# State-space rounds in a new order on all four engines, with the softplus head on ScalarE and the shift by columns

## The chip, the cores and the metric

The kernel runs on one core of a Trainium2 chip. The metric is device time in microseconds. A core has five engines that run side by side, each in the order of its own instruction list: TensorE (PE; PEld is its weight load), VectorE (DVE), ScalarE (ACT), GpSimd (POOL) and SyncE (SP, which issues the DMAs). They meet only at semaphores.

## The reference

Four stages follow each other, each with a layernorm in front and a residual behind: an attention-like recurrence over 32 sequences of 256 tokens and 128 features, a feed-forward net, a state-space block, and the feed-forward net again. The change concerns the state-space block, and the helper that ends a layernorm's statistics.

```python
zxbcdt = hidden_states @ W_in
z = zxbcdt[..., :D_INNER]
xBC = jax.nn.silu(_causal_dwconv(xBC, conv_w, conv_b))
...
dt = jax.nn.softplus(dt + dt_bias)
A = -jnp.exp(A_log)
y = _ssd(x, dt, A, Bm, Cm) + x * D[None, None, :, None]
y = y * jax.nn.silu(z)
y = y * jax.lax.rsqrt(jnp.mean(y * y, axis=-1, keepdims=True) + EPS) * norm_w
return y @ W_out
```

`_ssd` multiplies scores (products of the B and C features, times the exponential of a difference of running sums of dt*A) with x*dt, head by head. The depthwise convolution has 4 taps.

## The kernel before

The tokens stand in SBUF as 16 groups of 512 (4 tiles of 128). Every engine's program is written out by hand: stage by stage a function `space_half` (and `attention_half`, `ffn_half`) per engine lists what the engine does in one round. The order on an engine is the order of the code, and nothing reorders it.

**The state-space stage** has 16 rounds, h = 1 to 16. Round h works on three groups at once: b = h (projection and convolution), e = h - 1 (decays, scores, x*dt) and f = h - 2 (output, residual). Up to round 8 to 11 it also does the layernorm of a group x seven rounds ahead, turns it feature-major (`turn`), and projects dt for a group d = h + 6. The lines (of before) that matter:

- PE: `gate` L1974 (z), `conv` L1970, `log_decay` L1988 and L1990 (two fp16 matmuls: exponent of the decay, called ld below with head and batch), `head_outputs` L2001 (16 matmuls, called hy 0 and hy 1 for the two halves of the heads), `token_major` L2009, `transposes_of` L1645, `of_token` L1872 (dt), `steps_to_rows` L1962, `products` L2015, `mean_squares` L2023, `out_of` L2030.
- DVE: `stats_at` L1088 to L1093, `shift_at` L1100, `with_bias` L1401 (sets `z_done`), `taps` L1503 (three adds onto what ACT began), `times_dt` L1520, `skip` L1510, `mean_square` L1529, `add_residual` L1392 (the residual: 4 instructions), and the softplus chain of 64 columns for four groups at once (a quad), L1417 to L1452.
- ACT: `first_tap` L973 (begins a convolution block), `silu_x` L979, `silu_z` L984, `square_y` L989, `decay_of` L994, `products_out` L1000, `normalise_of` L823, `feature_major_of` L815, `exp_of_quad` L967. Two table loads a round, ahead of L994 and of L984.
- POOL: `score_of` L721 (4 a round), `gated_y` L727 (2), the sum of squares L768, `ln_rstd_of` L609 and L612, the rms root L777, and for a quad `diffs` (L739 to L745) and `split_sums` (L756 to L761).

The residual needs `out_of` (PE) and the root (POOL). The next round's hy 0 needs the residual, since both use the PSUM bank `y_bank[0]`. `skip(e, r)` needs hy r; `gated_y` needs `skip`; `square_y` needs `gated_y`.

**A quad's chain** runs over four rounds. In rounds 1, 5 and 9 `softplus_begin` makes -|z| and max(z, 0) on DVE, ACT takes the exponential, and `softplus_middle`, `_series` and `_end` follow on DVE. In rounds 2, 6 and 10 PE turns the steps (`steps_to_rows`, which waits for the end of the softplus chain and for this round's `with_bias`), DVE takes chunk sums (L1464; `products` waits for them, as they share `mid_bank[1]`), and POOL takes six steps of `diffs`. In rounds 3, 7 and 11 DVE runs two scans (`running_sums`, L1475 and L1476), and POOL six steps of `split_sums`.

`shift_at` is called in the attention stage as well, once for each of its groups:

```python
nc.vector.scalar_tensor_tensor(shift[u][:, :], mv[u][:, :, 0], -1.0, rstd[u][:, :],
                               ALU.mult, ALU.mult).then_inc(shift_done, 1)
```

## Time and profile before

| what | value |
|---|---|
| median of 3 runs | 834.76 us (832.9 to 836.47) |
| the profiled execution | 835.77 us, its span 833.7 us, mean granted clock 0.953 |
| busy: PE, DVE, ACT, POOL | 746.8, 619.6, 531.0, 556.2 us |
| attention, then feed-forward | until some 300 us, then until some 430 us |
| state-space rounds | some 430 to 735 us |
| second feed-forward | to the end |

The span runs from the first to the last instruction; the time has 2.07 us more around it. Busy time is what the profile draws; PE's is drawn too long, since the modelled end of a matmul lies behind the start of the next. A row of the timeline reads: start, length, engine, line, operation, names, shape, count, and in brackets how long the engine was idle before it and who ended that.

### The profile page before, as it was taken

The page shows a single profiled execution, that of the slowest core. Times are in us where ns is not written, and L with a number is a line of the kernel's source. Part 1 is how long each engine was busy: PE and PEld are TensorE (multiplying, and loading weights), DVE is VectorE, ACT ScalarE, POOL GpSimd, SP SyncE. Part 2 cuts the span into 40 slices and gives each one's busy share as a digit, 9 for nine tenths or more (in the row PEclk, how much of TensorE's full clock was granted, in tenths as well). Part 3 has the DMA queues.
Part 4 walks back from the last instruction along what each step waited for, and adds up shares of the span by engine and source line. Part 5 has one row for each costly group of instructions (what it writes and reads, how often), then busy time and mean ns, then how long its engine had stood idle before and what let it go on. Part 6 is the DMA issues. An engine that isn't in the chain of part 4 may idle for free. (4 is left out here: it accounts for less than half of the span.)

```text
span 833.7 us, 15931 instructions
## 1 busy us (share of the span) xinstructions
PE 746.8 (90%) x5114; PEld 547.7 (66%) x5114; DVE 619.6 (74%) x1728; ACT 531.0 (64%) x1023; POOL 556.2 (67%) x920
## 2 busy tenths in 40 slices
PE   3589999999999897999779799899979999979997
PEld 2578888888888775666644566566645565546665
DVE  3568877787788548888568787887888777668885
ACT  3244344434543236988548788788978688848886
POOL 1567666776677504777724697588758876777775
PEclk9689999999999899999759899999999999999999
DMA  4341131112111102000200000000000000000112
GB/s 126 82 134 46 50 77 34 30 30 48 39 30 30 29 15 102 0 1 0 78 3 7 1 1 9 1 1 5 7 1 1 9 1 1 1 1 27 51 51 77
DMA packets 59996, 25.83 MB, mean 31 GB/s; under 512 B 22288, under 2 KB 59152, under 8 KB 59664
## 3 DMA queue, kind: packets, MB, share of 16 engines
q1 hardware_dynamic: 59920, 24.90, 11.2%
q8 instruction: 37, 0.61, 0.3%
q14 instruction: 39, 0.32, 0.1%
HBM read 15.26 MB, written 9.63 MB: 30 GB/s over the span
## 5 line engine op out<-in xcount | busy, mean ns | idle before, releaser
L1503 DVE SCALAR_TENSOR_TENSOR arena<-bank,convw_sb,arena 128x510 f32<-128x510 f32 (+2 forms) x192 | 142.5, 745 | 31.9 <-ACT arena L973 27.2
L721 POOL TENSOR_TENSOR arena<-arena 128x768 f32<-128x768 f32 x64 | 114.8, 1814 | 12.8 <-ACT arena L1000 12.6
L701 POOL TENSOR_TENSOR arena<-ff,arena 128x512 f16<-128x512 f32 x64 | 73.6, 1159 | 28.7 <-ACT arena L938 26.6
L1970 PE MATMUL bank<-xnT,win_sb 128*128 128x512 f32 x128 | 73.9, 661 | 2.7 <-DVE arena L1503 2.7
L632 POOL TENSOR_TENSOR leafV<-leafV,leaf_tmp 32x14 f32<-32x14 f32 (+6 forms) x224 | 62.4, 278 | 17.6
L830 ACT ACTIVATE ff<-bank 128x256 f32<-128x256 f32 (+2 forms) x80 | 34.0, 424 | 57.6 <-PE bank L1658 35.3
L1324 DVE SCALAR_TENSOR_TENSOR ff<-bank,ff 128x512 f32<-128x512 f32 x96 | 64.5, 684 | 7.3 <-ACT ff L933 6.3
L933 ACT ACTIVATE ff<-bank 128x512 f32<-128x512 f32 x96 | 56.2, 587 | 18.4 <-PE bank L1886 18.0
L815 ACT ACTIVATE xnT<-bank 128x512 f32<-128x512 f32 x34 | 20.3, 597 | 73.3 <-PE bank L1645 73.3
L628 POOL TENSOR_TENSOR leaf_tmp<-leafV 32x14 f32<-32x14 f32 (+6 forms) x224 | 55.8, 249 | 16.4
L994 ACT ACTIVATE arena<-bank 128x384 f32<-128x384 f32 x128 | 59.8, 492 | 9.3 <-PE bank L1990 8.5
L2001 PE MATMUL bank<-arena 128*64 128x256 f32 (+1 forms) x512 | 49.7, 338 | 17.8 <-DVE x_all L1392 17.8
L727 POOL TENSOR_TENSOR arena<-arena 128x512 f32<-128x512 f32 x30 | 37.7, 1268 | 39.6 <-DVE arena L1510 39.4
L1128 DVE SCALAR_TENSOR_TENSOR arena<-bank,arena 128x256 f32<-128x256 f32 (+1 forms) x128 | 44.6, 411 | 25.8 <-PE bank L1732 15.7
L2001 PEld LDWEIGHTS bank<-arena 128*64 128x64 f32 x512 | 32.4, 139 | 45.3 <-DVE x_all L1392 22.9
L973 ACT ACTIVATE arena<-bank,convb_sb,convw_sb 128x512 f32<-128x512 f32 x64 | 49.9, 781 | 18.9 <-PE bank L1970 18.9
L823 ACT ACTIVATE xn<-x_all,shift,rstd 128x128 f32<-128x128 f32 x112 | 45.9, 481 | 11.4 <-DVE shift L1100 11.4
L692 POOL TENSOR_SCALAR xn<-x_all,pair_rstd,pair_shift 128x128 f32<-128x128 f32 x76 | 34.7, 467 | 23.2 <-DVE pair_shift L1299 20.4
L979 ACT ACTIVATE arena<-arena 128x512 f32<-128x512 f32 x64 | 38.6, 632 | 17.9 <-DVE arena L1503 17.9
L1988 PE MATMUL bank<-ff,slabs 128*128 128x384 f16 x128 | 41.0, 331 | 3.8 <-ACT arena L994 3.7
L938 ACT ACTIVATE arena<-ff 128x512 f16<-128x512 f32 x64 | 39.9, 623 | 6.1 <-DVE ff L1324 6.1
L1885 PE MATMUL bank<-xh,gate 128*128 128x512 f16 x96 | 36.8, 384 | 4.8 <-DVE x_all L1392 3.0
(216 smaller groups left out, 2162.5 us busy)
## 6 DMA issues: line engine op xcount, KB each, us to landing
LT_dram<-arena SPq DMA_DIRECT2D x16, 256.0 KB, 2.3
ff<-R_dram SPq DMA_DIRECT2D x16, 256.0 KB, 2.8
out<-x_all SPq DMA_DIRECT2D x8, 512.0 KB, 3.2
x_all<-in_L_attn_a_x SPq DMA_DIRECT2D x7, 512.0 KB, 5.6
slabs<-in_tables SPq DMA_DIRECT2D x2, 1024.0 KB, 6.0
ff<-in_tables SPq DMA_DIRECT2D x2, 768.0 KB, 4.3
x_all<-in_L_attn_a_x SPq DMA_DIRECT2D x2, 256.0 KB, 3.7
R_dram<-tab SPq DMA_DIRECT2D x2, 256.0 KB, 6.7
```

The lines of the kernel that those rows point to most:

```text
L628: nc.gpsimd.tensor_tensor(prod, V[:, s:s + 1, s + 1:LEAF].broadcast_to([leaf_rows, s, below]), V[:, 0:s, s:s + 1].broadcast_to([leaf_rows, ...
L632: nc.gpsimd.tensor_tensor(V[:, 0:s, s + 1:LEAF], V[:, 0:s, s + 1:LEAF], prod, ALU.subtract).then_inc(leaf_step, 1)
L701: nc.gpsimd.tensor_tensor(of_block(hl[u], j), hidT[u][:, j, :], of_block(hh[u], j), ALU.subtract).then_inc(hl_done[u], 1)
L721: nc.gpsimd.tensor_tensor(score[h], cb[g % 2], hgam[h], ALU.mult).then_inc(score_done, 1)
L823: last = nc.scalar.activation(xn[u][:, cols(t)], x_all[:, n % GROUPS * GROUP + t * P:n % GROUPS * GROUP + (t + 1) * P], ACT.Identity, scal ...
L933: nc.scalar.activation(silu_g[u][:, j, :], bank[u][(1, 3, 1)[j]][:, :], ACT.Silu, scale=DEQUANT).then_inc(silu_done[u], 1)
L973: nc.scalar.activation(xbc[r][b % 2], conv_bank[r % 2][:, :], ACT.Identity, scale=convw_sb[:, r, TAPS - 1:TAPS], bias=convb_sb[:, r:r + 1] ...
L994: nc.scalar.activation(hgam[h][:, batch * TRI:(batch + 1) * TRI], step_bank[batch][:, 0:TRI], ACT.Exp).then_inc(hgam_done, 1)
L1324: nc.vector.scalar_tensor_tensor(hidT[u][:, j, :], bank[u][(2, 0, 2)[j]][:, :], DEQUANT, silu_g[u][:, j, :], ALU.mult, ALU.mult).then_inc( ...
L1503: nc.vector.scalar_tensor_tensor(acc_of[:, :, s:SEQ], src_of[:, :, 0:SEQ - s], convw_sb[:, r, TAPS - 1 - s:TAPS - s], acc_of[:, :, s:SEQ], ...
L1970: mm(conv_bank[r % 2][:, :], win_sb[:, INNER + r * P:INNER + (r + 1) * P], xnT[b % XNT_SETS][:, :], start=True, stop=True).then_inc(conv_m ...
L2001: last = mm(y_bank[r][k * HEAD_DIM:(k + 1) * HEAD_DIM, batch * SEQ + c * P:(batch + 1) * SEQ], x_of[:, 2 * batch + c, h * HEAD_DIM:(h + 1) ...
```

## The change

In the state-space rounds, each engine's list is put in another order. Three instructions change their kind: -|z| and max(z, 0) of a quad become |z| (with the sign in the exponential's scale) and a Relu on ACT; `softplus_begin` leaves DVE's round. `shift_at` becomes four one-column instructions, everywhere it is called. The prologue keeps the old way for quad 0, and everything outside `space_half` and `shift_at` stays, but for the order of three SiLU operations ahead of the rounds.

```diff
 # POOL, space_half
                 if f is not None:
                     gated_y(f, 1)
+                if x is not None:
+                    ln_rstd_of(*x)
...
                 if e is not None:
                     score_of(e, 0)
-                    score_of(e, 1)
                 if f is not None:
                     pool.wait_ge(ms_done, done(f))
...
                 if e is not None:
+                    score_of(e, 1)
                     score_of(e, 2)
 # ACT
+            def softplus_begin(q):
+
+                act.wait_ge(z_done, done(QUAD * (q + 1) - 1))
+                act.wait_ge(chain_step, CHAIN * q)
+                nc.scalar.activation(nabs_dt[:, :], z_dt[q % 2][:, :], ACT.Abs).then_inc(chain_step, 1)
+                nc.scalar.activation(relu_dt[:, :], z_dt[q % 2][:, :], ACT.Relu).then_inc(chain_step, 1)
+                act.wait_ge(chain_step, CHAIN * q + 1)
+                nc.scalar.activation(e_dt[:, :], nabs_dt[:, :], ACT.Exp, scale=-1.0).then_inc(e_done, 1)
 # ACT, space_half: its whole order now
                     silu_x(e, 0)
                     silu_x(e, 2)
                     silu_x(e, 3)
+                if b is not None:
+                    first_tap(b, 0)
                 if turn is not None:
                     feature_major_of(*turn, mid_bank[0])
...
                     decay_of(e, 0, 1)
+                    decay_of(e, 0, 0)
                 if f is not None:
                     square_y(f, 0)
+                if e is not None:
+                    decay_of(e, 1, 1)
+                if exp_q is not None:
+                    softplus_begin(exp_q)
+                if e is not None:
+                    products_out(e, 1)
+                if f is not None:
                     square_y(f, 1)
...
                     silu_z(b, 1)
-                    first_tap(b, 3)
+                    silu_z(b, 0)
                     silu_x(b, 1)
-                    silu_z(b, 0)
 # DVE, shift_at
-                nc.vector.scalar_tensor_tensor(shift[u][:, :], mv[u][:, :, 0], -1.0, rstd[u][:, :],
-                                               ALU.mult, ALU.mult).then_inc(shift_done, 1)
+                for t in range(GROUP_TILES):
+                    last = nc.vector.tensor_scalar(shift[u][:, t:t + 1], rstd[u][:, t:t + 1], mv[u][:, t, 0:1], -1.0,
+                                                   ALU.mult, ALU.mult)
+                last.then_inc(shift_done, 1)
 # DVE, space_half
-                if begin_q is not None:
-                    softplus_begin(begin_q)
                 if chunk_q is not None:
                     chunk_sums(chunk_q)
-                if sums_q is not None:
-                    running_sums(sums_q)
...
+                if e is not None:
+                    times_dt(e, 0)
                 if f is not None:
                     mean_square(f)
-                if e is not None:
-                    times_dt(e, 0)
+                if sums_q is not None:
+                    running_sums(sums_q)
                 if b is not None:
                     taps(b, 2)
```

On PE a round now reads: gate 0, conv 0, hy 0, token-major 1, turn, ld(0,1), hy 1, ld(0,0), `of_token`, `steps_to_rows`, conv 1, ld(1,1), products 1, ld(1,0), products 0, ld(2,1), gate 1, conv 2, ld(2,0), token-major 0, ld(3,1), mean squares, ld(3,0), conv 3, `out_of`. Before, it read: gate 0, ld(0,1), hy 0, conv 0, hy 1, token-major 1, turn, ld(0,0), conv 1, `of_token`, `steps_to_rows`, ld(1,1), products 1 and 0, ld(1,0), ld(2,1), mean squares, gate 1, ld(2,0), token-major 0, conv 2, ld(3,1), ld(3,0), `out_of`, conv 3.

**DVE in round 5**, from the last group of taps ahead of the residual. Names are those of the program (`arena` holds the stage's tiles, `x_all` the tokens). Before:

```order
L1432 TENSOR_SCALAR dt_acc<-dt_w 128x64
L1439 SCALAR_TENSOR_TENSOR dt_acc<-dt_acc,dt_w 128x64 x3
L1392 SCALAR_TENSOR_TENSOR x_all<-bank_2,arena,x_all 128x128 x4
L1503 SCALAR_TENSOR_TENSOR arena<-bank_1,convw_sb,arena 128x2x255
L1503 SCALAR_TENSOR_TENSOR arena<-bank_1,convw_sb,arena 128x2x254
L1503 SCALAR_TENSOR_TENSOR arena<-bank_1,convw_sb,arena 128x2x253
L1439 SCALAR_TENSOR_TENSOR dt_acc<-dt_acc,dt_w 128x64 x3
L1446 SCALAR_TENSOR_TENSOR dt_acc<-dt_acc,dt_w 128x64
L1448 SCALAR_TENSOR_TENSOR dt_dt<-dt_acc,dt_relu 128x64
L1452 TENSOR_TENSOR dt_dA<-dt_dt,aneg_row 128x8x2x4
L1510 SCALAR_TENSOR_TENSOR arena<-arena,skip_col,bank_2 128x512
L1510 SCALAR_TENSOR_TENSOR arena<-arena,skip_col,bank_3 128x512
```

The same place with the change (residual L1403, taps L1514, `skip` L1521, `times_dt` L1531, series L1450):

```order
L1443 TENSOR_SCALAR dt_acc<-dt_w 128x64
L1521 SCALAR_TENSOR_TENSOR arena<-arena,skip_col,bank_2 128x512
L1531 TENSOR_TENSOR arena<-bank_3,dt_dt 128x4x128
L1450 SCALAR_TENSOR_TENSOR dt_acc<-dt_acc,dt_w 128x64 x6
L1457 SCALAR_TENSOR_TENSOR dt_acc<-dt_acc,dt_w 128x64
L1459 SCALAR_TENSOR_TENSOR dt_dt<-dt_acc,dt_relu 128x64
L1463 TENSOR_TENSOR dt_dA<-dt_dt,aneg_row 128x8x2x4
L1521 SCALAR_TENSOR_TENSOR arena<-arena,skip_col,bank_3 128x512
```

The whole chain now stands behind the residual and the last taps; its second part stands between `skip(e, 0)` and `skip(e, 1)`.

**ACT at the start of a plain round.** `bank_0` and `bank_1` are PSUM banks. Before, `first_tap(b, 0)` (L973) stands behind the squares and three decays:

```order
L994 ACT_TABLE_LOAD
L994 ACTIVATE arena<-bank_1 128x384
L815 ACTIVATE xnT<-bank_2 128x512
L989 ACTIVATE arena<-arena 128x512 x2
L994 ACTIVATE arena<-bank_0 128x384
L994 ACTIVATE arena<-bank_1 128x384
L973 ACTIVATE arena<-bank_0,convb_sb,convw_sb 128x512
L1000 ACTIVATE arena<-bank_3 128x384
```

With the change (`silu_x` L989, `first_tap` L983, `feature_major_of` L816, `decay_of` L1004):

```order
L994 ACTIVATE arena<-bank_3 128x512
L994 ACTIVATE arena<-bank_2 128x512
L989 ACTIVATE arena<-arena 128x512 x4
L983 ACTIVATE arena<-bank_0,convb_sb,convw_sb 128x512
L816 ACTIVATE xnT<-bank_2 128x512
L1004 ACT_TABLE_LOAD
```

`first_tap(b, 0)` now stands ahead of the table load, the decays and the squares.

**PE in round 6**, around `steps_to_rows` (L1962 before, L1971 with the change). Before:

```order
L1970 MATMUL bank_1<-xnT,win_sb 128x512
L1872 MATMUL bank_3<-win_sb,xnT 128x4 x4
L1962 MATMUL bank_3<-tab,dt_dA 32x128 x2
L1988 MATMUL bank_1<-ff,slabs 128x384
L1990 MATMUL bank_1<-never,ident 128x2x128
L2015 MATMUL bank_3<-arena 128x256
```

With the change:

```order
L1881 MATMUL bank_3<-win_sb,xnT 128x4 x4
L1971 MATMUL bank_3<-tab,dt_dA 32x128 x2
L1979 MATMUL bank_1<-xnT,win_sb 128x512
L1997 MATMUL bank_1<-ff,slabs 128x384
L1999 MATMUL bank_1<-never,ident 128x2x128
L2024 MATMUL bank_3<-arena 128x256
```

The convolution block 1 moved from ahead of `of_token` to behind `steps_to_rows`, that is behind its wait and ahead of the products.

## Rows read from the trace of the kernel before

**Rows 1.** Residuals of rounds 2, 5, 6, 7, 8 and 15: timeline of DVE

```profile
476.75 1.12 DVE L1392 SCALAR_TENSOR_TENSOR x_all<-bank,arena,x_all 128x128 f32<-128x128 f32 x4
...
534.75 1.12 DVE L1392 SCALAR_TENSOR_TENSOR x_all<-bank,arena,x_all 128x128 f32<-128x128 f32 x4
...
555.14 1.12 DVE L1392 SCALAR_TENSOR_TENSOR x_all<-bank,arena,x_all 128x128 f32<-128x128 f32 x4
...
574.39 1.12 DVE L1392 SCALAR_TENSOR_TENSOR x_all<-bank,arena,x_all 128x128 f32<-128x128 f32 x4
...
593.01 1.12 DVE L1392 SCALAR_TENSOR_TENSOR x_all<-bank,arena,x_all 128x128 f32<-128x128 f32 x4
...
720.64 0.60 DVE L1392 SCALAR_TENSOR_TENSOR x_all<-bank,arena,x_all 128x128 f32<-128x128 f32 x2
```

**Rows 2.** Stretch, length, busy (count) of PE PEld DVE ACT POOL, clock, DMA

```profile
687.04:703.84 16.80, 16.00 (x101) 10.05 (x100) 12.39 (x22) 13.80 (x25) 11.99 (x9) 1.00 0.01 1
...
574.39:593.01 18.62, 17.26 (x112) 11.46 (x112) 14.37 (x33) 16.03 (x30) 16.71 (x17) 1.00 0.04 11
514.02:534.75 20.73, 17.00 (x112) 11.47 (x112) 18.38 (x43) 18.79 (x36) 15.10 (x12) 1.00 0.01 2
...
651.30:670.24 18.94, 17.20 (x100) 10.59 (x99) 12.47 (x22) 13.37 (x24) 16.53 (x16) 0.91 0.04 10
```

**Rows 3.** Timeline of round 8, from the residual before it on

```profile
576.26 0.39 POOL L756 CAST pieces<-ff 32x256 f16<-32x256 f32 x1
...
578.07 1.52 PE L2001 MATMUL bank<-arena 128*64 128x256 f32 x16
579.64 0.75 DVE L1510 SCALAR_TENSOR_TENSOR arena<-arena,skip_col,bank 128x512 f32<-128x512 f32 x1 [1.26 <-PE bank L2001]
580.41 2.49 POOL L727 TENSOR_TENSOR arena<-arena 128x512 f32<-128x512 f32 x2
...
580.90 0.87 DVE L1088 BATCH_NORM_STATS2 stats<-x_all 128x6 f32<-128x128 f32 x4
...
582.93 0.63 ACT L989 ACTIVATE arena<-arena 128x512 f32<-128x512 f32 x1 [0.59 <-POOL arena L727]
...
584.21 0.78 ACT L973 ACTIVATE arena<-bank,convb_sb,convw_sb 128x512 f32<-128x512 f32 x1
...
585.02 2.31 DVE L1503 SCALAR_TENSOR_TENSOR arena<-bank,convw_sb,arena 128x510 f32<-128x510 f32 x3 [2.28 <-ACT arena L973]
```

**Rows 4.** Timeline of DVE and PE in rounds 5 and 6

```profile
532.42 1.15 DVE L1428 TENSOR_TENSOR dt_w<-dt_e,dt_rec 128x64 f32<-128x64 f32 x1
...
534.09 0.74 DVE L1439 SCALAR_TENSOR_TENSOR dt_acc<-dt_acc,dt_w 128x64 f32<-128x64 f32 x3
...
535.92 1.64 PE L2001 MATMUL bank<-arena 128*64 128x256 f32 x16 [3.68 <-DVE x_all L1392]
...
537.49 2.08 PE L1970 MATMUL bank<-xnT,win_sb 128*128 128x512 f32 x2
```

**Rows 5.** Timeline of POOL and DVE at the start of round 11

```profile
634.74 0.59 POOL L739 TENSOR_TENSOR ff<-ff 32x248 f32<-32x248 f32 x1
...
639.36 2.48 POOL L727 TENSOR_TENSOR arena<-arena 128x512 f32<-128x512 f32 x2
639.42 2.96 DVE L1475 TENSOR_TENSOR_SCAN ff<-ones_col,ff 32x256 f32<-32x256 f32 x1
```

**Rows 6.** The shift's line: durations ns min/median/max, first and last start

```profile
L1100 DVE SCALAR_TENSOR_TENSOR shift<-mv,rstd x28: 152/154/1165, 6.4 to 627.0; 128x4 f32<-128x4 f32 x28
```

**Rows 7.** Timeline of an attention round

```profile
209.04 0.28 DVE L1093 BATCH_NORM_AGGREGATE mv<-stats 128x2 f32<-128x6 f32 x3
...
210.80 0.15 DVE L1100 SCALAR_TENSOR_TENSOR shift<-mv,rstd 128x4 f32<-128x4 f32 x1
...
213.45 0.71 PE L1714 MATMUL bank<-ff,arena 128*128 128x128 f32 x4 [0.21 <-DVE arena L1170]
```

**Rows 8.** Who waited for DVE's L1170: us, times

```profile
  PE bank L1714: 2.9, 13
```

More of the change, by code:

```diff
@@ L2052, in space_half @@
                     gate(e, 0)
-                    if e > 0:
-                        quad_landed(e)
-                        log_decay(e, 0, 1)
+                if b is not None:
+                    pe.wait_ge(xnT_done, done(2 * GROUPS + b))
+                    conv(b, 0)
                 if f is not None:
@@ L2072, in space_half @@
                     if e > 0:
-                        log_decay(e, 0, 0)
-                if b is not None:
-                    conv(b, 1)
+                        quad_landed(e)
+                        log_decay(e, 0, 1)
+                if f is not None:
+                    pe.wait_ge(ms_done, past(f - 1))
+                    head_outputs(f, 1)
+                if e is not None and e > 0:
+                    log_decay(e, 0, 0)
                 if d is not None:
@@ L2084, in space_half @@
                     steps_to_rows(rows_q)
+                if b is not None:
+                    conv(b, 1)
                 if e is not None:
```

74 lines of the change are left out of this document (35 added, 39 removed).

## The prediction

> **What bounds the kernel now.** I read the page first: PE is busy 746.8 of 833.7 us (the table above). That is an average over stages with different limits, so I went on by stage, first to the stretches between residuals, then to the timeline of one round. The state-space rounds are measured from residual to residual: 476.75 to 720.64 us for the thirteen rounds 3 to 15, that is 243.9 us [rows 1]. Several kinds are seen there. A light round (13 to 15: no layernorm, no turn, no dt) takes 16.80 us with all engines partly idle: PE busy 16.00, ACT 13.80, DVE 12.39, POOL 11.99 [rows 2]. A full round takes 18.62 us (round 8), rounds 5 and 6, which carry the softplus chain, take 20.7 and 20.4, and round 7 takes 19.25 [rows 1, 2].
>
> The timeline of round 8 shows what sets the period [rows 3]. DVE waits twice: 1.26 us for the second head outputs before `skip(e,1)`, and 2.28 us for ACT's first tap before its own taps. The chain between the two is hy 1 (1.52), `skip` (0.75), two gated products on POOL (2.49), the square, two decays and the first tap on ACT (from 582.93 to 584.99), and from there DVE works without a gap to the residual (585.02 to 593.01 + 1.12), whose end releases hy 0. So the loop is residual, hy 0, conv, hy 1, skip, POOL, square, decays, first tap, taps, residual. No engine is full; a loop through all four is the bound. In round 8 POOL came late: it was at its six split steps from 576.26 and began the products only at 580.41, both at once, after `skip(e,1)`. Had the first been done by then, as in a round without split steps, the loop would be one product (1.25) shorter, some 17.4.
>
> The attention stage is another matter. In 13 rounds PE waits for DVE's L1170, 2.9 us in all and 0.21 in the round shown, and otherwise runs without a gap [rows 7, 8]. DVE works without a gap from the bias adds through the shift to L1170. So there every nanosecond added at the shift is added to the round.
>
> **The change part by part.**
>
> *First tap early (ACT), conv 0 ahead of hy 0 (PE).* The first tap no longer hangs on the square. It follows `silu_x(e,3)`, which needs the last taps (2.3 us behind the residual): ready at 2.25 + 0.63 + 0.78 = 3.7 us behind the residual's end, where DVE reaches its taps only after `skip(e,1)`, at 4.2 + 0.75 + 1.4 (statistics, 0.87 and the aggregates, and bias) = 6.35. The wait of 2.28 us is gone. Laid out from the residual's end with the durations above, DVE then needs 15.0 us for a full round. What is late next is PE: its list of a light round holds 16.00 us of drawn busy time [rows 2], of which tails of 0.07 to 0.16 at its five or six gaps are drawn too long; counted start to start I get 15.6, and 16.9 for a full round (17.26 drawn). The bounds are 15.2 and 16.0. I take 15.6 and 16.9. ACT (13.80 and 16.03 drawn) fits under both.
>
> So the thirteen rounds are laid out again, one by one, to be set against their 243.9.
>
> *Light rounds 13 to 15:* 15.6 each instead of 16.8, 46.8 in all. *Round 12* was 18.94, with the clock at 0.91 and POOL late by the split [rows 2]; with PE dense it goes to 15.7.
>
> *Rounds 4 and 8 (split steps on POOL):* these take 4.1 us (from 576.26 to the products at 580.41 [rows 3]) behind the last scores, and push the gated products, which are no longer in front of the taps. Behind a round as late as 3 and 7 below, PE starts at once: 16.7 and 16.6 (round 8 was 18.62).
>
> *Rounds 5 and 9:* 20.73 now [rows 2] in round 5, where -|z| and the chain's first half stand ahead of the residual. All of it leaves this round. ACT gets |z| and Relu, two of 64 columns, for which I take 0.25 each (a DVE instruction of that size takes that [rows 4]); products and gate 1 come 0.5 later, which PE's list hides; without that cover it would be 0.5 a round. 16.9 each.
>
> *Rounds 6 and 10:* the chain has only moved. The middle (five instructions, 1.55 us), six series steps and three of the end (nine at 0.25, 2.3 us; three take 0.74 [rows 4]), and one hold of 0.75 by POOL's gated product now lie in front of `skip(e,1)`: it starts at 8.1 instead of 4.2. Then statistics, bias at 10.2, and only then `steps_to_rows`, with conv 1 now between it and the products. PE is idle from 6.2 to 10.3. At the start of round 6 PE was idle 3.68 us, and the convolution behind the head outputs took 2.08 us, twice its usual time, at the lower of the two clock levels, 1.2 instead of 2.4 GHz [rows 4]. I expect the same fall here: conv 1 until 12.5, decay and products 14.4 instead of 7.1. From there the round is as usual, 9.2 to the residual: 23.6, where round 6 took 20.4. Without the fall of the clock it is 21.7.
>
> *Rounds 3, 7 and 11:* the scores end later on POOL (one more stands behind the root), so the six steps of `diffs` (4.6 us, 634.74 to 639.36 [rows 5]) end at 7.4, the gated products at 10.0, and now the first square stands ahead of a decay that gate 1 hangs on: everything comes 2.8 later. The running sums have moved from a place where DVE waited to one just ahead of the taps before the residual: 1.3 us, and up to 2.3 more if POOL holds them, as in round 11, where a scan of 0.65 took 2.96 behind two POOL instructions [rows 5]. I take 1.0 of hold (the root's length). 20.3 (round 3: 20.2, round 11, which has no dt and no statistics: 19.9), where round 7 took 19.25.
>
> *Sum over the rounds:* 20.2 + 16.7 + 16.9 + 23.6 + 20.3 + 16.6 + 16.9 + 23.6 + 19.9 + 15.7 + 46.8 = 237.2, against 243.9: 6.7 less. Rounds 1, 2 and 16 have a hold less on DVE and the same loops over a shorter way; I take 1.3 for them, an estimate. For waits that such a layout doesn't see I take off 0.6: **7.4 gained.** The bounds are 0 (another loop takes the place) and 16 (no fall of the clock, no hold).
>
> *The shift by columns.* In the state-space rounds, where a score runs on POOL, the shift takes up to 1.17 us instead of 0.15 [rows 6]. Four columns with one tensor input each may escape the hold. DVE no longer bounds these rounds, so this is hidden by PE's list; without that cover it would be up to 1.0 a round. In the attention rounds there is no hold and no cover. No row shows a one-column instruction with a per-partition operand. The nearest are the three small aggregates that take 0.28 us together where one takes 0.15 [rows 7]: each further one costs 0.065. Four columns then cost 0.2 more than one instruction, 13 times: **2.6 us lost.** From below nothing, if they cost no more than the one; from above 4 x 0.154 - 0.154 = 0.46, 13 times, 6.0.
>
> The Trainium skill (VectorE: DVE Perf Modes, "The DRAIN you can't avoid") says that the next Vector instruction does not start until the pipe of the last is empty. By it four columns cost four whole instructions, the 6.0 of the upper bound, and the whole sum would be a gain of 1.4. The rows at 0.065 apart speak against it.
>
> **Sum:** 7.4 - 2.6 = 4.8 us. The profiled execution goes from 835.77 to 831.0 (833.7 to 828.9 in its span); it is 1.0 above the median of 834.76, so the median goes to 830.0.
>
> **Rivals.**
> 1. *The clock does not fall and the scans are not held* (rounds 2, 6 and 10; 3, 7 and 11). For it: a round is full of matmuls on both sides of the idle time. Against it: that time is 4.1, longer than the 3.68 that it fell after. It gives 1.9 x 3 + 1.0 x 3 = 8.7 more: 821.
> 2. *The columns run one after another:* 6.0 in place of 2.6: 833.4. Against it the rows above, for it that page.
> 3. *POOL's loop takes the place of the one removed.* One score more stands behind the root, and the fourth score is needed by hy 1 of the next round; I find it done 0.4 us before that. If POOL's waits for the mean square are longer, the rounds stay as they are, and the columns cost 2.6: 837.4.
> 4. *Slower.* In rounds 2, 6 and 10 the chain in front of `skip(e,1)` meets holds at each of its three starts (a product of 64 columns took 1.15 instead of 0.25 [rows 4]), 2.0 more, and the idle PE falls to the low level for the products, gate and decays behind them too, 2.2 more: 4.2 x 3 = 12.6, 842.6. It decides from 3.0 us a round on; POOL, which is idle until `skip(e,0)`, speaks against the holds.
>
> **How the numbers follow.** A run of three resolves about 0.5% of this kernel, 4.2 us: faster is below 830.6, slower above 838.9. The forecast has 0.45 (its own range 826 to 834, half of it on each side of 830.6, a little more on the fast side), rival 1 0.20, rival 2 0.08, rival 3 0.10, rival 4 0.17. Faster: 0.26 + 0.20 = 0.46. Slower: 0.17. Same: 0.37. The range of 821 to 840 leaves out half of rival 1 and most of rival 4.
>
> **What would show it.** In the profile after: no wait for L983 (first tap) ahead of the first taps; light rounds of 15.6 with PE's idle time near nothing; rounds 5 and 9 near 17; round 6 and 10 near 23.6 with a lower clock, PE idle before `steps_to_rows`; round 7 at 20 with a first scan over 0.65; PE's wait for L1170's successor in attention at 0.41. The prediction is wrong if the light rounds stay at 16.8, if attention loses more than 4 us or nothing, or if round 6 is near 20.

## The result and the profile after

The changed kernel takes 831.86 us (median of 18 runs), the kernel before 836.62 beside it: a ratio of 0.9923, 95% interval 0.9905 to 0.9941. The ratio leaves out two of the 18 that ran in a slower state. The change makes the kernel faster by 0.6 to 0.95%. The forecast was 830.0, from 834.76: a gain of 4.8, and 4.8 is what the two medians give.

From the page of the changed kernel: its engines, and the group of the taps (columns: busy us, mean ns | idle time before it, and what ended most of that):

```profile
span 825.8 us, 16018 instructions
PE 738.0 (89%) x5114; PEld 545.4 (66%) x5114; DVE 618.8 (75%) x1806; ACT 529.0 (64%) x1029; POOL 557.7 (68%) x920
L1514 DVE SCALAR_TENSOR_TENSOR arena<-bank,convw_sb,arena 128x510 f32<-128x510 f32 (+2 forms) x192 | 142.5, 743 | 21.0 <-ACT arena L983 16.4
```

The span is 7.9 us shorter, and the page doesn't say where. (The profiled execution, 827.91 us, lies 4.0 below the median of its kernel and the one before 0.9 below its own, so 3.1 of the 7.9 belong to this pair of executions.) The residuals do, here those of rounds 2 and 15 in the timeline of DVE (before: [rows 1]):

```profile
482.53 1.12 DVE L1403 SCALAR_TENSOR_TENSOR x_all<-bank,arena,x_all 128x128 f32<-128x128 f32 x4 [0.56 <-PE bank L2142]
...
712.54 1.13 DVE L1403 SCALAR_TENSOR_TENSOR x_all<-bank,arena,x_all 128x128 f32<-128x128 f32 x4 [0.56 <-PE bank L2142]
```

The thirteen rounds take 230.0 us instead of 243.9, so 13.9 less; round 2's residual comes 5.8 later than before; the last two stretches of the stage together are 0.3 longer (26.75 instead of 26.46). 13.9 - 5.8 - 0.3 = 7.8, all but 0.1 of the 7.9. The 5.8 are lost before the state-space rounds begin. Rounds 4, 5, 6, 7, 8, 10 and 15 by window (columns as in [rows 2]):

```profile
501.31:518.47 17.16, 16.51 (x111) 11.38 (x112) 14.17 (x37) 14.87 (x29) 16.05 (x16) 1.00 0.05 11
518.47:535.07 16.60, 16.60 (x113) 11.48 (x112) 14.17 (x36) 16.01 (x33) 13.57 (x11) 1.00 0.01 1
535.07:557.71 22.64, 18.68 (x115) 12.39 (x114) 19.09 (x52) 15.80 (x30) 13.15 (x11) 0.92 0.00 1
557.71:576.51 18.80, 17.91 (x114) 11.46 (x112) 15.25 (x38) 16.70 (x31) 17.77 (x18) 1.00 0.00 1
576.51:593.68 17.17, 16.52 (x111) 11.39 (x112) 14.16 (x36) 14.87 (x29) 16.06 (x16) 1.00 0.05 11
...
610.28:630.61 20.33, 16.32 (x107) 10.71 (x106) 18.92 (x51) 15.81 (x30) 13.17 (x11) 1.00 0.00 1
...
697.05:712.54 15.49, 15.44 (x101) 10.06 (x100) 12.57 (x22) 13.82 (x25) 12.01 (x9) 1.00 0.00 1
```

In rounds 5 and 15 PE is busy for the whole window: it is the bound there. In round 6 it is not, and its clock is down (0.92). Round by round, in us from residual to residual, for all kernels of this study (each from one profiled execution; unchanged rounds repeat to 0.05 us between executions, but those in which the clock falls differ by up to 1.3):

| kernel | 3 | 4 | 5 | 6 | 7 | 8 | 9 | 10 | 11 | 12 | 13-15, mean | sum |
|---|---|---|---|---|---|---|---|---|---|---|---|---|
| before | 18.7 | 18.6 | 20.7 | 20.4 | 19.3 | 18.6 | 20.7 | 19.2 | 18.4 | 18.9 | 16.80 | 243.9 |
| predicted | 20.2 | 16.7 | 16.9 | 23.6 | 20.3 | 16.6 | 16.9 | 23.6 | 19.9 | 15.7 | 15.6 | 237.2 |
| changed | 18.8 | 17.2 | 16.6 | 22.6 | 18.8 | 17.2 | 16.6 | 20.3 | 18.4 | 17.0 | 15.49 | 230.0 |
| cols_alone | 18.3 | 18.5 | 20.7 | 21.3 | 18.3 | 18.5 | 20.7 | 18.0 | 19.6 | 16.9 | 16.80 | 241.0 |
| tap_early | 18.7 | 18.6 | 20.8 | 21.3 | 18.9 | 18.6 | 20.8 | 19.2 | 17.2 | 16.9 | 16.08 | 239.2 |
| tap_rstd | 18.1 | 18.0 | 20.9 | 20.4 | 18.6 | 17.8 | 20.9 | 19.4 | 17.1 | 16.9 | 16.09 | 236.2 |
| tap_rstd_cols | 18.1 | 17.8 | 21.1 | 20.4 | 18.6 | 17.8 | 21.1 | 19.4 | 17.1 | 16.9 | 16.09 | 236.4 |
| whole_shift | 19.5 | 17.8 | 16.6 | 24.0 | 19.5 | 17.8 | 16.6 | 20.3 | 18.4 | 17.1 | 15.49 | 234.0 |
| cols_space | 18.8 | 17.2 | 16.6 | 22.8 | 18.8 | 17.2 | 16.6 | 20.3 | 18.5 | 17.1 | 15.49 | 230.2 |
| conv0_late | 18.8 | 17.2 | 17.1 | 24.0 | 18.8 | 17.2 | 17.1 | 20.3 | 18.4 | 17.1 | 15.74 | 233.1 |
| conv1_first | 18.8 | 17.2 | 16.8 | 23.0 | 18.8 | 17.2 | 16.8 | 22.0 | 18.4 | 17.0 | 15.49 | 232.4 |
| chain_split | 18.8 | 17.2 | 21.3 | 19.9 | 18.8 | 17.2 | 21.3 | 18.1 | 18.4 | 17.0 | 15.49 | 234.4 |
| sums_first | 23.3 | 16.6 | 16.6 | 23.9 | 21.4 | 17.4 | 16.6 | 20.9 | 24.2 | 15.7 | 15.49 | 243.0 |
| tap_late | 25.0 | 18.9 | 22.4 | 25.1 | 22.6 | 19.7 | 19.1 | 26.2 | 19.4 | 24.3 | 19.25 | 280.5 |
| bias_early | 18.8 | 17.2 | 16.6 | 20.5 | 18.8 | 17.2 | 16.6 | 21.1 | 18.4 | 17.1 | 15.49 | 228.7 |

How large that is, round 6 shows. sums_first changes nothing in it, and in whole_shift the shift isn't held there (0.15 us at 544.70) and is followed by a wait of 2.24 for ACT. Yet both take 1.3 more than the changed kernel, at a lower mean clock, 0.86 for 0.92. Round 6 of whole_shift, then of sums_first:

```profile
529.99:553.95 23.96, 20.00 (x115) 13.26 (x114) 18.78 (x48) 15.81 (x30) 13.17 (x11) 0.86 0.00 1
539.19:563.11 23.92, 19.96 (x115) 13.20 (x114) 19.18 (x51) 15.79 (x30) 13.17 (x11) 0.86 0.00 1
```

conv0_late has 23.98 at 0.86 too, cols_space 22.77 at 0.93. So a difference of 1.3 in round 6 is no sign of what an edit does.

The attention stage went the other way. The shift's line, durations as in [rows 6], and an attention round in the timelines of DVE and PE:

```profile
L1110 DVE TENSOR_SCALAR shift<-rstd,mv x112: 201/203/215, 6.4 to 624.4; 128x1 f32<-128x1 f32 x112
```

```profile
113.06 0.57 DVE L1110 TENSOR_SCALAR shift<-rstd,mv 128x1 f32<-128x1 f32 x4
113.54 0.70 DVE L1164 STREAM_TRANSPOSE ff<-ff 128x512 f32<-128x512 f32 x1
...
115.53 0.41 DVE L1181 TENSOR_TENSOR arena<-arena,bank 128x256 f32<-128x256 f32 x1
...
116.00 0.71 PE L1723 MATMUL bank<-ff,arena 128*128 128x128 f32 x4 [0.37 <-DVE arena L1181]
...
133.04 0.71 PE L1723 MATMUL bank<-ff,arena 128*128 128x128 f32 x4 [0.37 <-DVE arena L1181]
```

and in the kernel before, at the same place of its round [rows 7]:

```profile
212.99 0.41 DVE L1170 TENSOR_TENSOR arena<-arena,bank 128x256 f32<-128x256 f32 x1
```

A column takes 0.203 us, the next begins 0.12 behind it, four take 0.57 where one instruction took 0.15. From the shift's start to that of the instruction PE waits for it is 2.47 us (113.06 to 115.53) instead of 2.19 (210.80 to 212.99): of the 0.42 that the columns add, 0.28 arrive, since the transpose and the reduction behind them take 0.13 less; why they do stays open. PE's wait is 0.37 instead of 0.21 [rows 7], and a round takes 17.04 us (116.00 to 133.04) instead of 16.76. From the first to the last of the thirteen waits, twelve rounds, it is 204.9 us, where the kernel before took 201.1: 3.8 lost, 0.65 in the first round and 0.28 to 0.29 in each other.

### The profile page after: what moved, and what is told of

Same layout as the page of the kernel before. It is cut to its first block and busy times, and to the rows that moved or that the text cites. A ratio compares the mean times of both kernels' runs of the same rounds, so it can differ in the third digit from the quotient of the medians.

```text
span 825.8 us, 16018 instructions
## 1 busy us (share of the span) xinstructions
PE 738.0 (89%) x5114; PEld 545.4 (66%) x5114; DVE 618.8 (75%) x1806; ACT 529.0 (64%) x1029; POOL 557.7 (68%) x920
## 5 line engine op out<-in xcount | busy, mean ns | idle before, releaser
L1514 DVE SCALAR_TENSOR_TENSOR arena<-bank,convw_sb,arena 128x510 f32<-128x510 f32 (+2 forms) x192 | 142.5, 743 | 21.0 <-ACT arena L983 16.4
L1979 PE MATMUL bank<-xnT,win_sb 128*128 128x512 f32 x128 | 71.8, 644 | 3.4 <-DVE arena L1514 3.3
L1004 ACT ACTIVATE arena<-bank 128x384 f32<-128x384 f32 x128 | 61.2, 492 | 17.5 <-PE bank L1999 17.2
L934 ACT ACTIVATE ff<-bank 128x512 f32<-128x512 f32 x96 | 56.2, 587 | 18.2 <-PE bank L1895 17.8
L983 ACT ACTIVATE arena<-bank,convb_sb,convw_sb 128x512 f32<-128x512 f32 x64 | 49.6, 774 | 25.5 <-PE bank L1979 21.3
L1139 DVE SCALAR_TENSOR_TENSOR arena<-bank,arena 128x256 f32<-128x256 f32 (+1 forms) x128 | 44.6, 411 | 25.8 <-PE bank L1741 15.6
L816 ACT ACTIVATE xnT<-bank 128x512 f32<-128x512 f32 x34 | 20.1, 594 | 64.9 <-PE bank L1654 64.9
L727 POOL TENSOR_TENSOR arena<-arena 128x512 f32<-128x512 f32 x30 | 37.8, 1269 | 23.3 <-DVE arena L1521 23.1
L1660 PE MATMUL bank<-ff,arena 128*128 128x64 f32 x256 | 36.2, 288 | 6.5 <-DVE ff L1164 6.5
```

The lines of the kernel that those rows point to most:

```text
L934: nc.scalar.activation(silu_g[u][:, j, :], bank[u][(1, 3, 1)[j]][:, :], ACT.Silu, scale=DEQUANT).then_inc(silu_done[u], 1)
L983: nc.scalar.activation(xbc[r][b % 2], conv_bank[r % 2][:, :], ACT.Identity, scale=convw_sb[:, r, TAPS - 1:TAPS], bias=convb_sb[:, r:r + 1] ...
L1004: nc.scalar.activation(hgam[h][:, batch * TRI:(batch + 1) * TRI], step_bank[batch][:, 0:TRI], ACT.Exp).then_inc(hgam_done, 1)
L1514: nc.vector.scalar_tensor_tensor(acc_of[:, :, s:SEQ], src_of[:, :, 0:SEQ - s], convw_sb[:, r, TAPS - 1 - s:TAPS - s], acc_of[:, :, s:SEQ], ...
L1979: mm(conv_bank[r % 2][:, :], win_sb[:, INNER + r * P:INNER + (r + 1) * P], xnT[b % XNT_SETS][:, :], start=True, stop=True).then_inc(conv_m ...
```

## The experiments

All of them compute the whole reference.

**cols_alone** and **whole_shift**: the columns alone, and everything but the columns. **cols_space**: the changed kernel with columns in the state-space stage only.

```diff
 # cols_space, shift_at of the changed kernel
+                if n < 2 * GROUPS:
+                    nc.vector.scalar_tensor_tensor(shift[u][:, :], mv[u][:, :, 0], -1.0, rstd[u][:, :],
+                                                   ALU.mult, ALU.mult).then_inc(shift_done, 1)
+                    return
                 for t in range(GROUP_TILES):
```

> The kernel before, with the shift by columns and nothing else of the change. Theory (the new order gives the gain, the columns cost): the period of the attention rounds goes from 16.76 to 17.05 us, as in the changed kernel (+3.7 over 13 rounds); in the state-space rounds the column form isn't held by GpSimd, so that rounds 3 to 10, where the shift lies on the loop, get 0 to 0.6 shorter each (2 in all): the span 1 to 3 us longer than before. Rival (the gain comes from the holds that the columns avoid): the state-space rounds get over 5 us shorter in all and the span shorter than before.

> The changed kernel with the shift as one instruction everywhere, as before the change. Theory: attention rounds back at 16.76 us, 3.7 to 4 us less; in the state-space rounds the shift is held by GpSimd again, up to 1 us a round, which TensorE's list hides for the most part: 0 to 2 us more. The span 2 to 4 us shorter than that of the changed kernel. Rival (the holds matter): state-space rounds 0.5 us longer each, no gain.

> The changed kernel with the columns in the state-space rounds alone, one instruction in the attention stage. Theory: attention rounds at 16.76 us, state-space rounds as in the changed kernel (light 15.5, full 16.6), so the span is 3.7 to 4 us shorter than that of the changed kernel, and the time 0.987 to 0.989 of before. Rival (the 0.285 us a round in attention come from something else in the change, the time of the statistics or a DMA): attention stays at 17.05.

cols_alone: 841.33 us, ratio 1.0049 (1.0017 to 1.0082). whole_shift: 827.72, ratio 0.989 (0.9848 to 0.9932). cols_space: 826.52, ratio 0.9877 (0.9844 to 0.991). From the first to the last of the thirteen waits in attention it is 204.91 in the first and 201.10 in the other two: the columns cost 3.8 there in whatever order. In the state-space rounds cols_alone is 2.9 shorter than the kernel before, but 2.1 of that lie in round 12, where the clock stays at 1.00 instead of 0.91. The rival, that the avoided holds are the gain, fell. In the new order one whole instruction instead of four columns costs 0.65 to 0.67 in each of rounds 3, 4, 7 and 8, 2.65 in all; the 1.3 in round 6 are the clock's (above). With the 3.8 of attention that would make whole_shift 1.2 shorter than the changed kernel; the interval of its four runs holds 0.9923 and doesn't decide it. In round 8 of whole_shift, first DVE, then POOL:

```profile
584.78 1.23 DVE L1109 SCALAR_TENSOR_TENSOR shift<-mv,rstd 128x4 f32<-128x4 f32 x1 [1.58 <-POOL rstd L612]
```

```profile
583.72 1.03 POOL L612 TENSOR_TENSOR rstd<-var_eps,half_neg 128x4 f32<-128x4 f32 x1
584.73 1.26 POOL L771 TENSOR_TENSOR arena<-arena 128x512 f32<-128x512 f32 x1
```

The shift waits for POOL's reciprocal deviation (`rstd`) and is let go as POOL starts on its next instruction, the sum of squares (L771). The two end together (586.01 and 585.99): the shift is held for all of that, 1.23 instead of 0.15. The columns take 0.58 at the same place (587.88 in the changed kernel, behind the same wait of 1.58).

**tap_early, tap_rstd, tap_rstd_cols**: the kernel before, with the first tap moved; then the reciprocal deviation ahead of the sum of squares as well; then the columns in the state-space stage too.

```diff
 # ACT (tap_early and on)
                     silu_x(e, 3)
+                    if b is not None and e > 0:
+                        first_tap(b, 0)
...
-                if b is not None and e != 0:
-                    first_tap(b, 0)
 # POOL (tap_rstd and on)
                     gated_y(f, 1)
+                if x is not None:
+                    ln_rstd_of(*x)
+                if f is not None:
                     pool.wait_ge(ysq_done, done(INNER_BLOCKS * f + 1))
                     nc.gpsimd.tensor_tensor(ysq[0][f % 2], ysq[0][f % 2], ysq[1][f % 2], ALU.add).then_inc(ysum_done, 1)
-                if x is not None:
-                    ln_rstd_of(*x)
```

> The kernel before, with first_tap(b, 0) moved on ScalarE to right behind the three SiLU, and nothing else of the change. Theory (the loop through the gated products, the square and this tap sets the period): light rounds go from 16.80 to 16.0 to 16.2 us (not 15.5, since conv 0 still stands behind the first head outputs), round 8 from 18.62 to 17.5, and the span gets 7 to 10 us shorter, as much as by the whole change or more, since neither the columns' cost nor the longer softplus round come with it. Rival (TensorE's new order is needed as well): light rounds stay over 16.5 and the span within 3 us of before.

> The kernel before with two moves: the first tap of block 0 right behind the SiLUs of x on ScalarE, and the layernorm's reciprocal deviation ahead of the sum of squares on GpSimd. The tap alone gave light rounds of 16.08 but left full rounds at 18.60, where the shift waited 1.10 us for that reciprocal and was then held 1.77 us by a score. Theory (two things stood behind the tap's wait, the place of the reciprocal and GpSimd's hold): the wait of 1.10 is gone, the shift of one instruction is still held; rounds 4 and 8 go from 18.6 to 17.5 to 18.2, light rounds stay at 16.08, sum of rounds 3 to 15 some 234 to 237. Rival (the loop through GpSimd and the square bounds the full rounds): they stay at 18.6.

> tap_rstd with the shift by columns in the state-space rounds alone. Theory: the hold is gone as well, full rounds 4 and 8 reach the 17.2 of the changed kernel, rounds 5 and 9 stay longer than its 16.6 since the softplus chain is still split, sum some 232 to 235; nearly the whole gain of the change is then in three of its moves. Rival (the rest of the new order carries the full rounds): 18 or more.

tap_early: 836.21 us, ratio 0.9992 (0.9967 to 1.0017). tap_rstd: 831.03, ratio 0.9935 (0.9904 to 0.9965). tap_rstd_cols: 833.91, ratio 0.9953 (0.992 to 0.9987), not to be told from tap_rstd. tap_early missed its forecast of 7 to 10 us: its thirteen rounds gain 4.7, and its runs show 2.8 at most. Some of the 4.7 is lost just ahead of them: from the statistics in round 1 to round 2's residual (440.11 to 478.01) it is 37.9 us at a mean clock of 0.86, where the kernel before took 35.4 at 0.90. With the tap alone the light rounds fall to 16.08, but round 8 stays at 18.6. In its timeline of DVE the wait of 2.28 for the tap [rows 3] is gone, and another has come:

```profile
584.68 2.30 DVE L1503 SCALAR_TENSOR_TENSOR arena<-bank,convw_sb,arena 128x510 f32<-128x510 f32 x3
588.09 1.77 DVE L1100 SCALAR_TENSOR_TENSOR shift<-mv,rstd 128x4 f32<-128x4 f32 x1 [1.10 <-POOL rstd L612]
```

The taps start 8.4 us into the round instead of 10.6. But they end at 586.98, and then come 1.10 of waiting and a shift of 1.77. In the kernel before it had no wait there and took 0.74 (587.25), so 2.1 of the 2.2 that were won are used up. The same place with tap_rstd:

```profile
582.55 2.30 DVE L1504 SCALAR_TENSOR_TENSOR arena<-bank,convw_sb,arena 128x510 f32<-128x510 f32 x3
584.77 0.15 DVE L1101 SCALAR_TENSOR_TENSOR shift<-mv,rstd 128x4 f32<-128x4 f32 x1
585.89 2.31 DVE L1504 SCALAR_TENSOR_TENSOR arena<-bank,convw_sb,arena 128x510 f32<-128x510 f32 x3 [0.97 <-ACT arena L974]
```

The shift has neither wait nor hold, though it is still one instruction, and so the columns have nothing left to give. That part of the theory, a hold that only the columns lift, fell. What the changed kernel has beyond that, 0.6 in light rounds, 0.7 in round 8 and 4.3 in rounds 5 and 9, belongs to the rest of the new order; the same rest costs 0.6 in round 3, 2.3 in round 6, 1.0 in round 10 and 1.3 in round 11.

**conv0_late** and **conv1_first**: on PE, conv 0 behind hy 0 again; conv 1 ahead of `of_token` and `steps_to_rows` again.

```diff
 # conv1_first, PE
+                if b is not None:
+                    conv(b, 1)
                 if d is not None:
...
                     steps_to_rows(rows_q)
-                if b is not None:
-                    conv(b, 1)
```

> The changed kernel with the first convolution of a round behind the first head outputs again, as before. Theory (light rounds of 15.49 have PE full because the convolution fills the time in which PE would wait for the residual): light rounds go to some 16.1, what tap_early alone reached, and PE's idle time before the first head outputs is 0.6 a round; full rounds, which wait on DVE, change by less than 0.3. Rival (the early tap alone fills PE, the place of the convolution is worth nothing): 15.5.

> The changed kernel with the second convolution ahead of the dt product and the turned steps, where PE waits idle in rounds 2, 6 and 10. Theory: in round 6 PE's wait of 3.04 us before the steps is shortened by the convolution's 0.96 at full clock or 1.9 at the lower clock level, round 6 goes from 22.64 to 20.7 to 21.7 and round 2 alike; the others stay within 0.2; median 1 to 3 us below the changed kernel's 831.9. Rival (that round is bound by DVE's list behind the chain, not by PE's work behind the steps): 22.6 as before.

conv0_late: 830.61 us in a single run, too little to set beside the changed kernel's median. PE waits 0.36 for the residual ahead of hy 0 in light rounds (669.10), and these take 15.74, between theory and rival: the place of conv 0 is worth 0.25 of the 0.6, and 0.35 come from the rest of the new order, which I didn't take apart. Rounds 5 and 9 take 0.5 more, so the place matters there too; the 1.3 more in round 6 are no sign of it (above). conv1_first: 831.86 us, ratio 0.9939 (0.9906 to 0.9971), the same as the changed kernel and against the theory: round 6 takes 22.97 instead of 22.64, and round 10 22.03 instead of 20.33. Round 10 in its timeline of PE, its start being 612.00:

```profile
621.39 0.38 PE L1971 MATMUL bank<-tab,dt_dA 128*32 128x128 f32 x2 [2.27 <-DVE dt_dA L1463]
...
623.80 1.28 PE L2024 MATMUL bank<-arena 128*128 128x256 f32 x4 [1.77 <-issue]
```

and in the changed kernel, from 610.28 on:

```profile
619.64 0.38 PE L1971 MATMUL bank<-tab,dt_dA 128*32 128x128 f32 x2 [3.11 <-DVE dt_dA L1463]
619.86 1.02 PE L1979 MATMUL bank<-xnT,win_sb 128*128 128x512 f32 x2
...
622.05 0.89 PE L2024 MATMUL bank<-arena 128*128 128x256 f32 x4 [0.90 <-issue]
```

```profile
621.27 0.69 DVE L1475 TENSOR_TENSOR_SCAN ff<-tab,bank 32x128 f32<-32x128 f32 x2
```

The products start 11.8 us into the round in both. In the code they wait for DVE's chunk sums (L1475), and in both they start 0.09 behind the end of these (621.96 here, 623.71 in conv1_first), though the profile names no releaser. So conv 1 costs nothing where it was put. Moved out, it leaves PE idle for another 0.9 ahead of the products, and the granted clock is 0.54 from 624 to 626 and 0.61 from 626 to 628, where it stays at 1.00 in the changed kernel: the products take 1.28 instead of 0.89. The loss in round 10 is that of the clock. That the place of conv 1 decides it isn't shown: tap_late aside, six kernels have conv 1 and the chain in this round where the changed kernel has them, and in four of them the clock stayed at 1.00 (20.33 or 20.34), in two it fell (sums_first 20.88 and bias_early 21.11, both at 0.92).

**chain_split**: the chain's middle and three of its steps on DVE ahead of the residual again.

```diff
+                if begin_q is not None:
+                    softplus_middle(begin_q)
+                    softplus_series(begin_q, 0, 3)
                 if f is not None and b is not None:
                     add_residual(f)
...
                 if begin_q is not None:
-                    softplus_middle(begin_q)
+                    softplus_series(begin_q, 3, 6)
+                    softplus_end(begin_q)
...
-                if begin_q is not None:
-                    softplus_series(begin_q, 0, 6)
-                    softplus_end(begin_q)
```

> The changed kernel with the middle and three steps of the softplus chain ahead of the residual again, the other three steps and the end behind it, as before; |z| and Relu stay on ScalarE. Theory (the chain only moved, but behind the residual it lies in front of the turned steps, where it makes PE idle long enough for the clock to fall): rounds 5 and 9 get some 2.3 longer (16.6 to 18.9), round 6 gets 2.3 shorter and another 1.0 to 1.5 since the clock stays (22.64 to some 19), round 10 gets 2.3 shorter (20.33 to 18); sum of rounds 3 to 15 within 2 us of 230.0, on the short side. Rival (the chain ahead of the residual costs more there than behind, since PE, ScalarE and GpSimd all wait for the residual): rounds 5 and 9 near 20.7 as before, the sum 3 or more longer.

838.49 us, ratio 1.0024 (0.9999 to 1.005). Rounds 5 and 9 take 4.7 more, 6 and 10 only 2.8 and 2.2 less. DVE at the end of round 5, and PE right behind it:

```profile
537.56 1.17 DVE L1439 TENSOR_TENSOR dt_w<-dt_e,dt_rec 128x64 f32<-128x64 f32 x1
538.77 1.73 DVE L1441 TENSOR_TENSOR dt_w<-dt_w 128x64 f32<-128x64 f32 x1
```

```profile
542.60 2.83 PE L2011 MATMUL bank<-arena 128*64 128x256 f32 x16 [4.15 <-DVE x_all L1403]
```

Ahead of the residual two small products are held for 2.4 us behind POOL's scores (535.06 to 540.41). In the changed kernel, behind the residual, they took 0.22 and 0.23 (539.42 and 539.68). And PE waits 4.15 for the late residual and runs the head outputs at the low clock, 2.83 where they take 1.52. The rival stands: the chain's place is worth 4.4 us in the thirteen rounds. By the runs (1.0024 beside 0.9923) the whole is more, some 8 us; rounds 1 and 2, which carry a quad's chain too, took 2.4 more in this execution, which is no more than executions differ by there, and the rest isn't placed.

**sums_first** and **tap_late**: the running sums ahead of the first taps again; the first tap behind the second square again, everything else as changed.

```diff
 # sums_first, DVE
+                if sums_q is not None:
+                    running_sums(sums_q)
                 if b is not None:
                     taps(b, 0)
...
-                if sums_q is not None:
-                    running_sums(sums_q)
```

> The changed kernel with the two scans of the running sums ahead of the first taps again, as before, instead of behind the mean square. Theory (in the new order DVE has no idle time in these rounds ahead of its taps, so the 1.34 us of scans cost their length at either place): rounds 3, 7 and 11 within 0.3 of 18.79, 18.80 and 18.41. Rival (the scans' old place is a place where DVE waits, their new one is on the path to the residual): 0.5 to 1.3 shorter.

> The changed kernel with the first tap of block 0 on ScalarE behind the second square again, all else as changed. Theory (the early tap is the move that the others need, since without it the loop through hy 1, the products on GpSimd, the square and the tap sets every round): light rounds 16.8 or longer, since one more decay, the softplus head and a products' copy now stand ahead of the square, full rounds 18.6 or longer, sum 243 or more. Rival (the other moves carry a part of the gain alone): light rounds 16.1 to 16.5, sum 235 to 240.

sums_first: 841.26 us in a single run, and both theories were wrong: rounds 3, 7 and 11 take 4.5, 2.6 and 5.7 more. DVE and POOL in its round 7:

```profile
571.44 2.96 DVE L1486 TENSOR_TENSOR_SCAN ff<-ones_col,ff 32x256 f32<-32x256 f32 x1 [0.39 <-POOL ff L745]
```

```profile
570.69 0.72 POOL L745 TENSOR_TENSOR ff<-ff 32x256 f32<-32x256 f32 x1
571.37 2.48 POOL L727 TENSOR_TENSOR arena<-arena 128x512 f32<-128x512 f32 x2
```

A scan that waits for POOL's last step is let go just as POOL begins its two gated products, and is held through both. The whole round is 2.6 longer. In the new place, behind the mean square, all four scans of this line take 0.669 us (573.14 in round 7). POOL's root ran beside them there (573.30), and it was the root that became longer, 1.32 instead of 1.03.

tap_late: 882.74 us in a single run, 46 more than before. The theory (light rounds 16.8 or longer, the sum 243 or more) held, by far more than it said: 19.25 and 280.5. In its round 14 DVE waits 3.12 us for the tap, where the kernel before waits 2.87 (at 696.51). PE then waits for those taps ahead of conv 2, which goes to the same bank, and runs it at a lower clock, 1.56 instead of 1.02:

```profile
738.84 4.53 DVE L1513 SCALAR_TENSOR_TENSOR arena<-bank,convw_sb,arena 128x510 f32<-128x510 f32 x6 [3.12 <-ACT arena L983]
...
741.21 1.56 PE L1978 MATMUL bank<-xnT,win_sb 128*128 128x512 f32 x2 [2.05 <-DVE arena L1513]
```

So the early tap is what the other moves need; without it they lose.

**bias_early**: cols_space, and in rounds 2 and 6 `with_bias` on DVE behind the chain's end and ahead of `skip(e, 1)` and the statistics.

```diff
-                if d is not None:
+                if d is not None and chunk_q is None:
                     with_bias(d)
...
                     softplus_end(begin_q)
+                    if d is not None and d + 1 < GROUPS:
+                        with_bias(d + 1)
                 if e is not None and e < GROUPS - 1:
                     skip(e, 1)
```

> cols_space (the changed kernel with the shift by columns in the state-space rounds alone) with one move more: in rounds 2 and 6 the dt bias stands on DVE behind the end of the softplus chain and ahead of the second skip and the statistics, instead of behind both. Theory (PE waits 3.04 us in round 6 for that bias, and its clock falls): the turned steps start some 1.7 us earlier, PE waits some 1.3 us there, the clock stays at 1.00 and the second convolution takes 1.02 us instead of 1.92; round 6 goes from 22.77 to 19.8 to 20.6, round 2 gains as much, the other rounds within 0.1 of cols_space. Sum of rounds 3 to 15 some 227.8, time 4 to 5 us under cols_space: a ratio of 0.981 to 0.985 to the kernel before. Rival (the round is bound by DVE's own list, which the move doesn't shorten): round 6 at 22 or more, ratio 0.987.

821.63 us (6 runs), ratio 0.9826 (0.9801 to 0.985), the fastest of all and as the theory had it. Round 6 takes 20.45 with the clock at 1.00; round 10, in which nothing was moved, takes 21.11, which the last section comes back to. PE there, first in the changed kernel, then in bias_early:

```profile
546.31 0.59 PE L1971 MATMUL bank<-tab,dt_dA 128*32 128x128 f32 x2 [3.04 <-DVE dt_z L1412]
546.68 1.92 PE L1979 MATMUL bank<-xnT,win_sb 128*128 128x512 f32 x2
```

```profile
539.58 0.38 PE L1977 MATMUL bank<-tab,dt_dA 128*32 128x128 f32 x2 [1.21 <-DVE dt_z L1416]
539.79 1.02 PE L1985 MATMUL bank<-xnT,win_sb 128*128 128x512 f32 x2
```

## Why the prediction came out

The number was right, 830.0 for 831.86, and the mechanisms of the light rounds, of rounds 5 and 9 and of the loss in attention were too. That the sum came out is luck in part: the gain in the rounds and the loss ahead of them were both forecast too small, and within the rounds errors of both signs cancelled.

- **Light rounds and PE as the next bound:** right. 15.49 for 15.6. The early first tap alone gives 16.08; conv 0 and PE's list give the rest.
- **Rounds 5 and 9, the chain leaves them:** right, 16.60 for 16.9. The price on ACT was right too: |z| and Relu take 0.248 and 0.246 us for 0.25.
- **Rounds 4, 8 and 12:** in the step "push the gated products, which are no longer in front of the taps" only block 0 is out of their way. Two things still stand behind them. One is the reciprocal deviation, for which the shift waits 1.58 in round 8. The other is ACT's first tap of block 1, behind both squares: it ends at 587.96 in round 8, so without the first wait the second would have left all but 0.4 of it. Round 12 has no shift, and there the tap alone makes DVE wait 3.34:

```profile
587.18 0.78 ACT L983 ACTIVATE arena<-bank,convb_sb,convw_sb 128x512 f32<-128x512 f32 x1
...
657.89 0.63 ACT L999 ACTIVATE arena<-arena 128x512 f32<-128x512 f32 x1 [1.83 <-POOL arena L727]
...
660.50 2.31 DVE L1514 SCALAR_TENSOR_TENSOR arena<-bank,convw_sb,arena 128x510 f32<-128x510 f32 x3 [3.34 <-ACT arena L983]
```

  17.2 for 16.7 and 16.6, and 17.0 for 15.7 in round 12. The layout's condition, a late round ahead, didn't come either; in sums_first, where it did, rounds 4 and 12 take 16.6 and 15.7 as forecast, and round 8 17.4.
- **Round 6:** the layout held. From the residual's end (536.20) `skip(e, 1)` starts at 8.0 (predicted 8.1), the bias ends at 10.0 (10.2), the clock falls, conv 1 ends at 12.4 (12.5) and the products at 14.8 (14.4). From there to the residual's end it is 7.9, not the 9.2 of a usual round: 22.6 for 23.6. In other executions of this round the low clock lasted longer, and 24.0 came out.
- **Round 10:** wrong. It was laid out like round 6, but there is no group d = 16: no dt product and no bias, so that what is said ahead of the prediction of the steps' wait for `with_bias` holds for rounds 2 and 6 alone. The steps wait only for the chain, PE's clock stayed, and it took 20.3 for 23.6.
- **"I take 1.0 of hold" for the running sums in rounds 3, 7 and 11:** wrong, and with it that they "have moved from a place where DVE waited". DVE waited there only as long as the tap was late. In the new order the old place costs 12.9 us over the three rounds, and the new one meets no hold. The layout up to the gated products held (in round 7 they end 9.6 behind the residual's end, 10.0 forecast); 0.4 to 0.5 a round stay unplaced. 18.8, 18.8 and 18.4 for 20.2, 20.3 and 19.9.
- **Rounds 1, 2 and 16, 1.3 gained:** not seen. From the statistics in round 1 to round 2's residual it is 35.1 us (from 447.42) instead of 35.4 (from 441.38), at a clock of 0.95 and 0.90, and the end of the stage is 0.3 longer. Between executions that first stretch takes from 35.1 to 37.5 in the new order and from 35.4 to 37.9 in the old, tap_late (39.5) aside.
- **Columns in attention, 2.6:** mis-sized, 3.8 between the first and the last wait. A column starts 0.12 behind the last, not 0.065, and the one instruction was followed after 0.07 (210.80 to 210.87), not after its 0.15. That "every nanosecond added at the shift is added to the round" was wrong the other way: it was 0.28 of 0.42. Before round 2's residual it may be more: kernels with columns in attention have it at 482.0 to 485.8, those without at 476.1 to 481.7. The upper bound of 6.0, by which no column starts before the last has ended, is the one that the rule of the Trainium skill (VectorE: DVE Perf Modes, "The DRAIN you can't avoid") gives, taken by itself: the next instruction starts when the pipe is empty. The same section adds that a next instruction which isn't held starts earlier. The rows show a column starting 0.12 into one of 0.203, so the measurement decides against the rule as a price here.
- **"DVE no longer bounds these rounds, so this is hidden by PE's list"**, said of the shift's hold: wrong in rounds 3, 4, 7 and 8, where whole_shift loses 2.65 us; right in 5, 6, 9 and 10.
- **Rival 1** (no fall of the clock, scans not held) is what happened in part: scans not held at all, and the clock fell in round 6 but not in round 10. Rival 3 did not occur.
- **Its signs:** the first taps of a light round follow without a wait (687.71), those of block 1 wait 1.12 for ACT (691.13); PE's wait in attention is 0.37 for 0.41. The loss there, 3.8, came close to the 4 at which the prediction called itself wrong.

In sum: rounds 3 to 15 gained 13.9 instead of 6.7. Of these 7.2, 4.4 lie in rounds 3, 7 and 11, 3.3 in round 10, 1.0 in round 6 and 0.9 in rounds 5, 9 and 13 to 15, less 2.4 in rounds 4, 8 and 12. Outside them 1.9 was to be lost (1.3 - 0.6 - 2.6); in this pair of executions it was 6.1: 3.8 for the columns in attention, 1.9 ahead of the first of those waits (64.50 for 62.61; the kernels of this study have it between 62.4 and 65.3, with columns or without), 0.3 at the end of the stage, and 0.1 elsewhere. The change is two changes of opposite sign. Without the columns in attention it is worth 0.9 to 1.6% (cols_space), and tap_rstd, two moved lines of it, reaches about what all of it does (0.9935 beside 0.9923): it has less of the gain and none of the columns' cost.

## What to carry to other kernels

When a wait on a loop is removed, list what the waiting instruction hid, on every engine: here the removal of one tap's wait gave nothing in full rounds until a second value came earlier too, and a scan's cheap old place became the most expensive one. An instruction of DVE that waits for POOL was released here just as POOL started on its next work, the worst moment for a hold (1.23 for 0.15, 2.96 for 0.67); put it where its value has long been ready, or where POOL waits. And before a difference between two profiles is put down to an edit, look at the same stretch in a kernel whose edit doesn't touch it. A helper that is called in two stages is to be priced in each, and split if they differ.

## What the runs showed of the hardware

- Within POOL's holds the form matters: in the same place four one-column instructions with one tensor input and a per-partition operand took 0.58 us together, a two-tensor instruction of four columns 1.23 (1.77 in tap_early).
- A scan of DVE was held through two instructions of POOL, one behind the other: 2.96 beside 2.48 (sums_first).
- How long the clock stays low after the same wait differs. In round 6 PE waits 3.04 in the changed kernel and in whole_shift, and the conv behind takes 1.92 in both. Then the first products take 1.12 and the second 0.82 in the changed kernel (548.92, 550.15), 1.49 and 1.49 in whole_shift (543.86, 545.67): 1.3 us of the round.
- The clock after a wait of PE is not decided by the wait alone. In round 10 PE waited 3.11 us in the changed kernel and its clock stayed at 1.00. In bias_early, whose instructions are the same there, it waited 3.13, the mean clock of the round was 0.92, and it took 21.11 for 20.33. Its rounds 6 and 10:

```profile
530.14:550.59 20.45, 17.35 (x115) 11.68 (x114) 19.03 (x52) 15.81 (x30) 13.19 (x11) 1.00 0.00 1
603.15:624.26 21.11, 17.90 (x107) 11.37 (x106) 18.94 (x51) 15.81 (x30) 13.19 (x11) 0.92 0.00 1
```

  Why it fell in the one and not in the other stays open; a gain that hangs on it should be counted as a chance.
